# A graph layer and a routed feed-forward on one core: the copies of sorted rows are queued one third earlier, the last visits' pieces come ahead of the last two nodes' steps, the pads go two pieces later, and the rows get a fourth buffer

## The reference

```python
msgs = layernorm(x)[edge_src] * edge_weight[:, None]
agg  = segment_sum(msgs, edge_dst)              # 12500 x 256
x    = x + agg @ W.T + b
h    = layernorm(x)
idx, prb = argmax / max of softmax(h @ gate_w + gate_b)     # one expert for each row
pos  = how many earlier rows chose the same expert; kept = pos < C   # C = 1954
y    = (relu(buf[idx] @ w1[idx] + b1[idx]) @ w2[idx] + b2[idx]) * prb * kept
out  = x + y
```

## Time and profile before

| | us |
|---|---|
| median of 3 runs | 2306.87 |
| lowest, highest | 2302.67, 2307.46 |
| the profiled execution | 2304.34 |
| its span, first to last instruction | 2302.5 |
| mean granted TensorE clock | 0.892 |

### The profile page before, as it was taken

One profiled execution on the slowest core, in us unless ns is written; L12 is line 12 of the kernel. 1 busy time (PEld: TensorE's weight loads), 2 busy tenths in 40 slices (PEclk: granted clock), 3 DMA queues, 4 the chain that ended last, 5 costly groups with the idle time before them and its releaser, 6 DMA issues.

```text
span 2302.5 us, 36668 instructions
## 1 busy us (share of the span) xinstructions
PE 1777.4 (77%) x9852; PEld 1173.6 (51%) x9852; DVE 1241.0 (54%) x6358; ACT 990.2 (43%) x1941; POOL 1701.1 (74%) x1774
## 2 busy tenths in 40 slices
PE   4444456665999887877887877877988888887899
PEld 3222234343666654545544545545655555555798
DVE  8977433444666555445445445445545555554553
ACT  6777423343555443333333333333444444444222
POOL 7777777777777777777777777777777777775465
PEclk9999985655999998888988888888999999998899
DMA  7766346667777776657557576756776676766478
GB/s 252 230 218 214 115 139 189 197 203 269 237 245 237 242 253 181 206 170 260 168 169 258 166 249 180 243 173 199 235 251 216 180 251 207 257 218 209 138 250 323
DMA packets 172806, 494.76 MB, mean 215 GB/s; under 512 B 48181, under 2 KB 86837, under 8 KB 149894
## 3 DMA queue, kind: packets, MB, share of 16 engines
q0 software_dynamic: 84960, 231.11, 34.0%
q1 hardware_dynamic: 70404, 235.95, 30.2%
q10 hardware_dynamic: 17234, 25.32, 3.0%
HBM read 596.46 MB, written 141.13 MB: 320 GB/s over the span
## 4 chain that ended last, share of the span: by engine, by line
POOL 34%; PE 32%; issue 14%; DVE 11%; ACT 6%; DMA 1%; ACTq 1%; SPq 0%; DVEq 0%; POOLq 0%
POOL msg L744 34%; PE ps L1094 12%; PE ps L1124 11%; PE ps L1112 3%; PE ps L1103 2%; DVE hmid L1515 1%; ACT hmid L916 1%; PE ps L1062 1%; PE ps L1011 1%; ACT hmid L911 1%; ACT hf L901 1%; DVE aggT L1525 1%; DVE st L1423 1%; DVE xrow L1421 1%; DVE onehot L1344 1%
## 5 line engine op out<-in xcount | busy, mean ns | idle before, releaser
L744 POOL DMA_INDIRECT msg<-normed,src_sb x1457 | 1397.8, 959 | 443.9 <-issue 442.3
L1094 PE MATMUL ps<-wsl,hTf 128*128 128x512 f32 x680 | 415.6, 767 | 57.5 <-ACT hTf L906 57.5
L1002 PE MATMUL ps<-msg,onehot 128*32 128x256 f32 x3322 | 312.7, 445 | 164.2 <-DMA msg<-normed,src_sb 94.8
L1124 PE MATMUL ps<-wsl,hmid 128*128 128x256 f32 x1680 | 392.0, 387 | 15.4 <-ACT hmid L916 15.4
L1124 PEld LDWEIGHTS ps<-wsl,hmid 128*128 128x128 f32 x1680 | 314.2, 192 | 65.2 <-issue 25.7
L1515 DVE TENSOR_TENSOR hmid<-ps,wsl 128x512 f32<-128x512 f32 x210 | 142.5, 690 | 342.8 <-PE ps L1103 307.4
L1094 PEld LDWEIGHTS ps<-wsl,hTf 128*128 128x128 f32 x680 | 161.2, 250 | 258.0 <-issue 184.7
L868 ACT COPY pairs<-ps 128x256 f32<-128x256 f32 x208 | 77.4, 372 | 446.4 <-PE ps L1002 436.1
L1002 PEld LDWEIGHTS ps<-msg,onehot 128*32 128x32 f32 x3322 | 116.3, 120 | 287.0 <-DMA msg<-normed,src_sb 109.8
L1011 PE MATMUL ps<-shift,pairs 128*128 128x96 f32 x832 | 167.9, 334 | 109.4 <-ACT pairs L868 108.8
L1372 DVE TENSOR_TENSOR aggT<-aggT,ps 128x192 f32 x208 | 73.5, 353 | 318.8 <-PE ps L1011 301.6
(11 more groups left out here) (148 smaller groups left out, 2551.3 us busy)
## 6 DMA issues: line engine op xcount, KB each, us to landing
wsl<-in_wsecond SPq DMA_DIRECT2D x105, 1152.0 KB
wsl<-in_wfirst SPq DMA_DIRECT2D x105, 1028.0 KB
rows_by_expert<-tiles_by_expert SPq DMA_DIRECT2D x752, 130.0 KB
msg<-normed,src_sb POOLq DMA_INDIRECT x1457
xrow<-in_x SPq DMA_DIRECT2D x97, 128.0 KB
wsl<-in_x SPq DMA_DIRECT2D x24, 512.0 KB, 4.0
normed<-wsl ACTq DMA_DIRECT2D x24, 512.0 KB, 3.2
tiles_by_expert<-srow ACTq DMA_DIRECT2D x94, 130.0 KB
```

The source lines that it names most:

```text
L744: pool.indirect_dma_start(out=msg[:, chunk.at + j, :], out_offset=None, in_=x if k < RAW else ln_dram, in_offset=bass.IndirectOffsetOnAxis ...
L1002: last = nc.tensor.matmul(ps[h * QWIN:(h + 1) * QWIN, t % 2, 0:D], onehot[:, j, :], msg[:, j, :], start=i == 0, stop=i == chunk.quarters[h ...
L1094: last = nc.tensor.matmul(ps[:, H + half, :], hTf[:, k, :], w1_at(v % 2)[:, k, half * HALF * P:(half + 1) * HALF * P], start=k == 0, stop= ...
L1124: last = nc.tensor.matmul(ps[:, Y, 0:D], hmid[:, c, :], w2_at(v % 2)[:, c, :], start=c == 0, stop=c == FC - 1)
```

## The change

Four edits, all of them to places in the list but one. `HBUFS` goes from 3 to 4. In the main loop `cp` of a node comes at the end of its fifth slot (behind `tn`) and not near the start of its sixth. In the closing list the norm, turn and logits of nodes 96 and 97 go behind `hl`, `hn` and `tf` of visit 85 and around `l2` of visit 84; their choice, ranks and route go behind `l1` of 85; and `pads` goes behind `l2` of 86, where it stood ahead of `l1` of 85. The plans of the visits after 88 move with them.

```diff
-HBUFS = 3
+HBUFS = 4
...
-        if stage[6] is not None and stage[6] < c - 1:
-            events.append(("cp", stage[6]))
...
         if stage[2] is not None:
             events.append(("tn", stage[2]))
+        if stage[5] is not None and stage[5] < c - 1:
+            events.append(("cp", stage[5]))
         for v in plan_at.get(t, ()):
             plan(v, t)
...
-    events += [("gnn", a), ("gnn", b), ("ra", c), ("x2", a), ("x2", b), ("rk", c), ("st", a), ("st", b), ("nn", a),
-               ("nn", b), ("rb", c), ("l1", first), ("tn", a), ("tn", b), ("th", first)]
+    events += [("gnn", a), ("gnn", b), ("ra", c), ("x2", a), ("x2", b), ("rk", c), ("st", a), ("st", b), ("rb", c),
+               ("l1", first), ("th", first)]
     for v in plan_at.get(real, ()):
         plan(v, real)
-    events += [("lg", a), ("lg", b)]
     for do in ("hl", "hn", "tf"):
         once(do, second)
-    events += [("l2", first), ("ra", a), ("ra", b), ("z", first), ("rk", a), ("rk", b), ("rb", a), ("rb", b)]
+    events += [("nn", a), ("nn", b), ("l2", first), ("tn", a), ("tn", b), ("z", first), ("lg", a), ("lg", b)]
     queue.pop(0)
     once("hl", queue[1][0])
-    events.append(("pads",))
+    rest()
+    events += [("ra", a), ("ra", b), ("rk", a), ("rk", b), ("rb", a), ("rb", b)]
+    rest()
     planned = full
...
     for _ in range(AHEAD):
         plan_last()
+    rest()
+    rest()
+    events.append(("pads",))
```

More of the change, by code:

```diff
@@ L169, in schedule_of @@
             continue
-        stage = [starts.get(t - s) for s in range(7)]
+        stage = [starts.get(t - s) for s in range(6)]
         for v, at in queue:
```

## The result

| | us |
|---|---|
| changed kernel, median of 4 runs | 2442.7 (2439.83 to 2452.92) |
| kernel before on the same chip, median of 4 | 2307.16 |
| ratio, 95% interval | 1.0589 (1.0562 to 1.0616) |
| profiled execution, its span | 2452.92, 2451.1 |
| mean granted TensorE clock | 0.864 (before 0.892) |

A forecast was written before the change was run, and what follows sets the result against it. POOL's gathers were taken to set the main loop's pace, with PE bounding the visits from 2170 us. Terms 45.3 (visits 19 to 53) + 3.2 (later stretch) + 3.2 (closing part) = 51.7 us slower: 2358.5 us, range 2312 to 2392.

The forecast's parts named there:

- The mechanism in the main loop: Visits 19 to 53: row loads issued behind the copies land late, ACT's norm and PE wait, and POOL is 42 us late.
- the early nodes, cost at nothing: Copies of nodes 0 to 32, before the visits summed from 19 on: the forecast gave them no loss.
- the sum 45.3 us for visits 19 to 53: Main loop: norm late by 0.97 us in 26 periods with skipped `wa`, 2.23 us in 9 with a real one.
- L: Time from issue to landing of a visit's rows: taken as 3.1 us with a skipped `wa`, 4.1 us with a real one.
- the later stretch, 3.2 us: Five visits on four nodes, behind visit 54: 19.2 us of delay, of which PE's 16.0 us waits for gathers take all but 3.2.
- The closing part, 3.2 us: Closing part up to visit 88: loses 4.7 us by the pads less 1.5 us gained, ends -4 and +8.
- The pads' term: Closing part: pads issued ahead of the rows of 88 make `wb` to norm 12.5 us instead of 7.85, 4.7 us more.
- The gain of 1.5 us: Closing part: new order of visits 84 and 85 gains 1.5 us up to `z` of 86, ends -4 and +2.
- The fourth buffer at nothing: Main loop: the fourth buffer costs and gives nothing, since no row load waits for a buffer in the trace.
- Quiet landing: Rival: rows land in 2.2 us as in a quiet queue, only the closing part's 3 us is lost, 2310 us; chance 0.12.
- the other sign: Rival: quiet landing in the loop and a closing part that gains by filling PE's wait, 2301 us; chance 0.07.
- heavier: Rival: real weight loads and copies fill the queue, landing over 5.5 us in periods with real `wa`, about 2410 us; chance 0.08.

The follow-up runs named there:

- cp_early: Kernel before with only the copies of nodes 0 to 32 moved to their new place behind the fifth slot's turn: 2344.04 us, 1.0166 against the kernel before.
- cp_late: Kernel before with only the copies of nodes 33 to 93 moved to their new place: 2394.69 us, 1.0396 against the kernel before.
- short_late_2: Kernel before with copies of 48 instead of 128 rows, those of nodes 33 to 93 moved: 2337.16 us, 1.0123; short copies unmoved 2306.39 us.
- closing_alone: Changed kernel with the copies back at their old place, keeping four buffers and the new closing order: 2311.4 us, 1.0028 against the kernel before.
- cp_alone: Kernel before with only the copies moved, in the whole loop; three buffers, old closing part: 2441.36 us, 1.0605 against the kernel before.
- short_copies_before: Kernel before with copies of 48 instead of 128 rows, on the slow chip: 2908.52 us, 0.9993 against the kernel before there.
- short_copies_late: Kernel before with copies of 48 rows, those of nodes 33 to 93 moved, on the slow chip: 2900.32 us, 0.9976 against the kernel before there.

## Why the prediction was right or wrong

**The mechanism in the main loop was right.** Each sign that I named for it came: the load 8.5 us behind `wa`, ACT's norm waiting for rows, PE's longer wait for the norm (3.3 us a period, from 1.6), POOL waiting for PE. The last gather is late too, but by 130 us and not by 40. Of the two signs for the closing part one came, the rows of 88 behind the pads, and one did not, PE's wait before node 96.

**Step that failed first: the early nodes, cost at nothing.** I worked out the period of visit 34 and began my sum at visit 19. For nodes 0 to 31 the queue's order is another: `load_x` stands where the visit's rows stand later, and the copies overtake that, 32 loads in all. Worth 41 us, by cp_early and by DVE's waits, and half of the miss of 84 us. The rows that would have told me are the SP lines of the kernel before, `wa`, residual rows, copies, at 696 us and, inside the gap of the earlier trace rows, again at 741 us; I looked at that stretch only for landing times. The orders of SP shown with the change are of the middle alone.

**Second: the sum 45.3 us for visits 19 to 53.** It came to 75.9 us in the trace (126.2 less 50.3). Two terms:
- L behind a skipped `wa` was 3.65 us (3.01 to 4.13), not 3.1; behind a real one 4.38 (3.98 to 5.04), not 4.1. The delays were 1.58 us, not 0.97, and 2.37, not 2.23: 26 x 1.58 + 9 x 2.37 = 62.4 us. I had weighed 3.83 us against 2.22 and took a value between them; the row of the same situation, copies straight ahead with gathers running, was nearly right as it stood.
- The way from a norm to the next `wa` was held constant, without a reason. It grew from 11.10 to 11.48 us, 35 times: 13.2 us. The granted clock of this stretch is 0.86 (869 to 1720 us) against 0.88, with PE idle more between visits; its first-layer matmuls take 951 ns in the mean from 900 to 1600 us, 896 before. Two more traces go the same way: cp_late has 11.40 us with 938 ns at a clock of 0.85, short_late_2 11.09 us with 899 ns at 0.88 (900 to 1600 us; the kernel before 0.87, the changed one 0.85). That the clock does it is read from these rows; no run changes the clock alone.

**Third: the later stretch, 3.2 us.** From visit 54 to 84 it is 17.9 us more (16.3 in cp_late). I had let PE's 16.0 us of waiting for gathers take all but 3.2 of 19.2 us. In the changed kernel PE waits for no gather from 1760 to 2220 us, so these 16 us were used up, but the delay is there all the same: ACT waits 24.9 us for rows in this stretch, in 17 norms, and POOL, from 1720 to 2232 us, waits for PE:

```profile
POOL msg L748 <- PE ps L1006: 17.9, 10, 3.1
```

What failed is the overlap: I took PE's delay as hidden by waits for POOL, as if POOL kept its pace, but POOL was held up by PE. No run takes this stretch by itself; cp_late, which holds it and the loop, loses 91 us where the two terms gave 48.5.

**A slip in the sum.** It adds the whole 45.3 us, though the sentence on POOL has only 42 us left of them behind its slack of 3.05 us. Rightly added up, the forecast would have been 3 us lower, further off.

**The closing part, 3.2 us, was 8.1** (3.5 to 9.7 by the interval). The pads' term was right (`wb` to norm 12.98 us in closing_alone, 12.07 in the changed kernel, 12.5 forecast: 4.2 to 5.1 us more than before). The gain of 1.5 us did not come; the waits of closing_alone listed above, the last one aside, are 10.5 us, where the kernel before had 10.3 (7.09 + 2.03 + 1.20).

**The fourth buffer at nothing** was not tried alone, but in cp_alone, with three buffers, SP waits at no row load for a buffer from 560 to 2320 us, so there is nothing for it to give in the loop. The parts sum to 138 + 8 us and the whole is 135.5. The intervals of the two large ones are some 6 us to each side, so that is at the edge of the noise; whether something overlaps stays open.

**The rivals.** Quiet landing fell with L, and so did the other sign; heavier, 2410 us, was nearer to the 2442.7 than the forecast, by luck, for its reason did not come: its L of over 5.5 us came in no real period of visits 19 to 53 (at most 5.04). L falls from 3.57 to 2.87 us with the copies' bytes (short_late_2). The Trainium skill ("DMA: Bandwidth & Descriptors", Queues, rings and completion order) has a completion wait for earlier writes of its DMA engine; the fall of L agrees, but does not prove it. The loads behind copies took 3.65 us here. The other figure of the Trainium skill (the same page, Anatomy of one DMA), which it gives for GpSimd's path and by which I estimated 2.3 us for 130 KB, does not fit that.

## What to carry to other kernels

When one issue moves in an in-order queue, list what it overtakes in every phase of the program, not in one period, and look at who waits for each of those. If the overtaken load sits in a loop through other engines (here load, norm, matmul, relu, next issue), its delay is paid in every turn. Take its landing time from a row with the same bytes ahead of it and the same traffic beside it. And before you let a wait of one engine for another hide a delay, ask whether the other still keeps its pace. Here, moving the small loads ahead as well gave the whole loss back.

## What the runs showed of the hardware that I had not expected

- A load of 128 x 260 numbers lands in 2.2 us in the quiet queue (one row of the kernel before), 2.87 us behind eight copies of 49 KB, 3.57 us behind eight of 130 KB (`wa` skipped), though SP needs 6.3 us to issue these eight in either case.
- The same program, kernel before, takes 2303 to 2308 us in the median on the other chips and 2912 us on another, at a granted clock of 0.82 from 900 to 1600 us (short_copies_before), and there a reordering that costs 1.3% elsewhere can't be seen (short_copies_late against short_copies_before).
